# Norm statistics packed into column quarters of one PSUM bank, earlier first norm, W_proj sums in the free bank, in a gated recurrent layer with a ternary MLP

## The reference

```python
x = x + attn(layernorm(x))      # W_r, W_i: 1024 x 1024
x = x + ffn(layernorm(x))       # W_fc: 4096 x 1024, W_proj: 1024 x 4096
# attn
r = sigmoid(x @ W_r.T); i = sigmoid(x @ W_i.T)
log_a = 8 * r * log_sigmoid(lambd)
h[t] = exp(log_a) * h[t-1] + sqrt(1 - exp(2*log_a)) * (i * x)
# ffn, absmean: W / mean(|W|), rounded and clamped to -1, 0, 1
h = gelu(x @ absmean(W_fc).T)
h = layernorm(h) * ln_w + ln_b          # over 4096
y = h @ absmean(W_proj).T
```

## Time and profile before

| | us |
|---|---|
| median of three runs | 1408.09 |
| lowest run | 1407.48 |
| profiled execution | 1406.31 |
| its span (slowest core) | 1404.8 |
| spans of the eight cores | 1399.6 to 1404.8 |
| PE busy | 1260.0 |
| DVE busy | 860.9 |
| ACT busy | 746.0 |

### The profile page before, as it was taken

How to read it: one execution, slowest core, us unless ns; L and a number is a source line. 1 busy time by engine, 2 the same in 40 slices (tenths; PEclk the granted TensorE clock), 3 DMA queues, 4 the chain that set the end, 5 groups by cost and what they waited for, 6 DMA issues and landing times.

```text
span 1404.8 us, 18437 instructions; the slowest of 8 cores (1399.6 to 1404.8 us)
## 1 busy us (share of the span) xinstructions
PE 1260.0 (90%) x6180; PEld 545.5 (39%) x6180; DVE 860.9 (61%) x1554; ACT 746.0 (53%) x1155; POOL 9.1 (1%) x20
## 2 busy tenths in 40 slices
PE   2734775969999999999999999999999999999998
PEld 0211232424434444444434444444444443444443
DVE  4588676766366755677366745676457736676333
ACT  2678955861547634672647444763557354761320
POOL 2000000000000000000000000000000000000000
PEclk8866898979999999999999999999999999999999
DMA  9954763431100210002000110012000210000001
GB/s 165 312 183 112 231 196 120 151 127 46 38 1 9 58 57 1 1 24 88 10 1 8 61 53 1 1 38 83 1 0 24 61 38 1 8 24 30 1 23 38
DMA packets 32780, 85.11 MB, mean 61 GB/s; under 512 B 4016, under 2 KB 4016, under 8 KB 32688
## 3 DMA queue, kind: packets, MB, share of 16 engines
q1 hardware_dynamic: 30384, 79.74, 17.8%
q0 software_dynamic: 2304, 4.20, 2.0%
HBM read 71.34 MB, written 16.78 MB: 63 GB/s over the span
## 4 chain that ended last, share of the span: by engine, by line
PE 71%; DVE 11%; ACT 10%; issue 7%; DMA 1%; DVEq 0%; SPq 0%; ACTq 0%
PE gp L405 26%; PE yp L537 26%; PE gp L290 12%; ACT qi L607 2%; PE pS L430 1%; PE yp L225 1%; DVE acc L590 1%; PE yp L226 1%; DVE t_q L348 1%; DVE gsq_f L421 1%; PE pQ L430 1%; ACT g_f L415 1%; ACT gp L308 1%; DVE t_q L345 1%; DVE ln L274 1%
## 5 line engine op out<-in xcount | busy, mean ns | idle before, releaser
L537 PE MATMUL yp<-g_f,wp_f 128*128 128x512 bf16 x2048 | 462.7, 383 | 27.3 <-DVE cw L797 27.3
L405 PE MATMUL gp<-ln,wfc_f 128*128 128x512 bf16 x2048 | 466.4, 383 | 3.0 <-DVE wfc_f L609 3.0
L415 ACT ACTIVATE g_f<-gp 128x512 bf16<-128x512 f32 x256 | 151.9, 596 | 387.8 <-PE gp L405 385.0
L537 PEld LDWEIGHTS yp<-g_f,wp_f 128*128 128x128 fp8e4 x2048 | 201.6, 99 | 277.9 <-issue 44.1
L405 PEld LDWEIGHTS gp<-ln,wfc_f 128*128 128x128 fp8e4 x2048 | 198.5, 99 | 258.6 <-issue 31.1
L421 DVE TENSOR_TENSOR gsq_f<-g_f 128x512 bf16<-128x512 bf16 x256 | 108.6, 424 | 240.6 <-ACT g_f L415 239.9
L290 PE MATMUL gp<-ln,wr_q 128*128 128x512 bf16 x512 | 127.9, 389 | 20.9 <-DVE ln L274 12.2
L290 PE MATMUL gp<-ln,wi_q 128*128 128x512 bf16 x512 | 125.2, 389 | 1.7 <-DVE t_q L333 1.7
L302 ACT ACTIVATE gp<-gp 128x1024 f32<-128x1024 f32 x64 | 64.5, 1008 | 82.6 <-PE gp L290 82.6
L460 DVE TENSOR_SCALAR g_f<-g_f,lnw_pp 128x512 bf16<-128x512 bf16 x256 | 86.9, 347 | 24.3 <-PE pQ L430 24.3
L215 ACT ACTIVATE stx<-xb 128x512 bf16<-128x512 f32 x112 | 69.3, 619 | 34.0 <-DVE xb L356 34.0
(11 more groups left out here) (120 smaller groups left out, 1012.4 us busy)
## 6 DMA issues: line engine op xcount, KB each, us to landing
wp_f<-wp SPq DMA_DIRECT2D x41, 512.0 KB, 5.3
y<-xb SPq DMA_DIRECT2D x64, 256.0 KB, 2.2
xb<-x SPq DMA_DIRECT2D x48, 256.0 KB, 3.1
ln<-wp SPq DMA_DIRECT2D x10, 512.0 KB, 4.4
xb<-x SPq DMA_DIRECT2D x8, 512.0 KB, 6.9
wfc_f<-wfc SPq DMA_DIRECT2D x8, 512.0 KB, 18.6
g_f<-wfc SPq DMA_DIRECT2D x8, 512.0 KB, 18.4
wp_f<-wfc SPq DMA_DIRECT2D x8, 512.0 KB, 18.4
```

Of the source, the lines that this page charges most:

```text
L405: fn = lambda E, d=d: E.matmul(bank(h % 4), wfc_q[:, h * D + d * 128:h * D + (d + 1) * 128], ch(ln[k % 2], d), start=(d == 0), stop=(d == ...
L415: gelu_tok[(k, h)] = p.op("scalar", lambda E: E.activation(ch(g_sb, h), bank(h % 4), AF.Gelu))
L537: fn = lambda E, kh=kh: E.matmul(pY[b][:, :], wp_q[:, (d * NH + kh) * 128:(d * NH + kh + 1) * 128], ch(g_sb, kh), start=(kh == 0), stop=(k ...
```

## The change

- Norms 1 and 2 collect their sums as norm 3 does: `stat_pair` takes two chunks and does four matmuls with a 128 x 32 ones matrix, the two copies into rows 0 to 63 of one bank and the two squares into rows 64 to 127. Norm 3's `stat3` uses the same layout and so only `pS`.
- A new step adds the quarters: `sums_out`, one ACT copy of the bank, and `sums_mm`, two fp32 matmuls of 64 rows each, into the sum bank and the square bank. It replaces `sums3_out` and `sums3_mm`, and is new for norms 1 and 2.
- Norm 1 in the feed: the preparations run at n = 0 to 7 without pauses, the pairs at n = 2, 4, 6, 8, `sums_out` at 9, `sums_mm` at 10, `rows_var` at 11, `rows_rs` at 13, `rows_b` at 14, and the halves spread so that they end at h = 30 (from h = 15, one a group, where n is h).
- Norm 2: the pairs stand in steps e = 4 and 6, behind the last half, and behind matmul 26 of projection group 4; `sums_mm` stands behind that group.
- `cw_mm` and `cw_out` take several d at once and use `pQ`; they stand at e = 3 (d = 0), e = 5 (1 to 3) and behind the last half (4 to 7).
- The first norm of all (k = 0, norm 1) stays with `stat_mm`.

```diff
+    def stat_pair(preps, c, buf, free):
+        p.wait("tensor", *preps[c][1:], *preps[c + 1][1:], tok_ones)
+        if c == 0:
+            p.wait("tensor", *free[0])
+        for first, src in ((0, stx), (64, stq)):
+            for j in range(2):
+                sl = preps[c + j][0]
+                fn = lambda E, first=first, src=src, j=j, sl=sl: E.matmul(
+                    buf[first + 32 * j:first + 32 * j + 32, :], ones_bf[:, 0:32], ch(src, sl),
+                    start=(c == 0), stop=(c == ND - 2))
...
+        st_use[0] = st_use[1] = tk
+    def sums_out(tok_stat, buf, dst, old):
+        p.wait("scalar", tok_stat, *old)
+        return p.op("scalar", lambda E: E.activation(dst[:, :], buf[:, :], AF.Copy))
+    def sums_mm(tok, src, bS, bQ, free):
+        p.wait("tensor", tok, *free[1])
+        p.quiet("tensor", lambda E: E.matmul(bS[:, :], ones_f[0:64, :], src[0:64, :], start=True, stop=True))
+        return p.op("tensor", lambda E: E.matmul(bQ[:, :], ones_f[64:128, :], src[64:128, :], start=True, stop=True))
...  gate_step
+        if e in (4, 6):
+            stat_pair(prep2, e - 4, pS, s_free)
...
-        if e >= 3:
-            stat_mm(prep2[e - 3], e - 3, pS, pQ, s_free)
...  stat3
+        for n in (0, 2):
+            for first, src in ((0, lambda j: ch(g_sb, 4 * b + j)), (64, lambda j: ch(gsq, j))):
+                for j in (n, n + 1):
+                    at = first + 32 * (j - n)
...  feed
-                if n in PREP_AT:
-                    c = PREP_AT[n]
-                    prep1[c] = stat_prep(ln1_next, c, x_tok[(ln1_next, c)])
-                if n - 2 in PREP_AT:
-                    c = PREP_AT[n - 2]
-                    tok_st1 = stat_mm(prep1[c], c, pY[0], pY[1], y_free)
-                if n == 13:
-                    var1 = rows_var(tok_st1, pY[0], pY[1], y_free, D, rs_t, mb_t, applied)
-                if n == 15:
-                    rows1 = rows_rs(var1, rs_t)
-                if n == 16:
+                if n in (2, 4, 6, 8):
+                    tok_st1 = stat_pair(prep1, n - 2, pY[0], y_free)
+                if 0 <= n < ND:
+                    prep1[n] = stat_prep(ln1_next, n, x_tok[(ln1_next, n)])
+                if n == 9:
+                    rows1 = sums_out(tok_st1, pY[0], rs_t, applied)
+                if n == 10:
+                    rows1 = sums_mm(rows1, rs_t, pY[0], pY[1], y_free)
+                if n == 11:
+                    rows1 = rows_var(rows1, pY[0], pY[1], y_free, D, rs_t, mb_t, applied)
+                if n == 13:
+                    rows1 = rows_rs(rows1, rs_t)
+                if n == 14:
                     rows_b(rows1, rs_t, mb_t)
                     fill = apply_halves(ln1_next, 1)
-                for _ in range(-(-len(fill) // (NH - h))):
-                    fill.pop(0)()
+                if n > 14 and fill:
+                    for _ in range(-(-len(fill) // (NH - 1 - h))):
+                        fill.pop(0)()
...  k = 0
-    tail_stat(prep2, 5)
+    stat_pair(prep2, 4, pS, s_free)
     gate_tail(0, prep2, "vector")
-    tail_stat(prep2, 6)
-    st2 = tail_stat(prep2, 7)
+    st2 = sums_out(stat_pair(prep2, 6, pS, s_free), pS, rs_t, applied)
+    st2 = sums_mm(st2, rs_t, pS, pQ, s_free)
...
+    def cw_mm(*ds):
+        p.wait("tensor", *s_free[1])
+        for d in ds:
+            p.wait("tensor", *[wp_ready[i] for i in range(4 * d, 4 * d + 4)], tok_lnwb)
...  (into pQ[:, 4 * d:4 * d + 4])
+    CW_AT = {3: (0, 1), 5: (1, 4)}
...  k >= 1
-        tail_stat(prep2, 5)
+        stat_pair(prep2, 4, pS, s_free)
         gate_tail(k, prep2)
         y_part(k - 1, 4, 0, 9)
         evac(k - 1, 3)
-        tail_stat(prep2, 6)
-        y_part(k - 1, 4, 9, 20)
-        if k == 1:
-            cw_out(5, cw_mm(5))
-        st2 = tail_stat(prep2, 7)
-        y_part(k - 1, 4, 20, NH)
+        y_part(k - 1, 4, 9, 26)
+        st2 = sums_out(stat_pair(prep2, 6, pS, s_free), pS, rs_t, applied)
+        y_part(k - 1, 4, 26, NH)
+        st2 = sums_mm(st2, rs_t, pS, pQ, s_free)
         r2 = rows_a(st2, pS, pQ, s_free, D, rs_t, mb_t, applied)
```

More of the change, by code:

```diff
@@ L227, in stat_mm @@
         return st_use[sl]
+    def stat_pair(preps, c, buf, free):
[8 more added lines that the diff above has]
+                    start=(c == 0), stop=(c == ND - 2))
+                if first and j:
+                    tk = p.op("tensor", fn)
+                else:
+                    p.quiet("tensor", fn)
+        st_use[0] = st_use[1] = tk
+        return tk
+    def sums_out(tok_stat, buf, dst, old):
[5 more added lines that the diff above has]
+        return p.op("tensor", lambda E: E.matmul(bQ[:, :], ones_f[64:128, :], src[64:128, :], start=True, stop=True))
     def rows_var(tok_stat, bS, bQ, free, n, RS, MB, old):
@@ L427, in stat3 @@
             p.wait("tensor", *s_free[0], *s_free[1])
[L428 to L435, removed]
+        for n in (0, 2):
+            for first, src in ((0, lambda j: ch(g_sb, 4 * b + j)), (64, lambda j: ch(gsq, j))):
+                for j in (n, n + 1):
+                    at = first + 32 * (j - n)
+                    fn = lambda E, at=at, j=j, m=src(j): E.matmul(
+                        pS[at:at + 32, :], ones_bf[:, 0:32], m,
+                        start=(b == 0 and j < 2), stop=(b == NH // 4 - 1 and j >= 2))
+                    if first and j == 3:
+                        tk = p.op("tensor", fn)
+                    else:
+                        p.quiet("tensor", fn)
         for j in range(4):
@@ L438, in stat3 @@
             st3_tok[(k, 4 * b + j)] = tk
[L440 to L452, removed]
     def rows3(tok):
@@ L778, in wp_quant, with cw_out @@
         wp_reloads()
[L780 to L790, removed]
-                p.quiet("tensor", fn)
-        return tk
-    def cw_out(d, tk):
-        b = d % 2
+    def cw_mm(*ds):
+        p.wait("tensor", *s_free[1])
+        for d in ds:
+            p.wait("tensor", *[wp_ready[i] for i in range(4 * d, 4 * d + 4)], tok_lnwb)
+            for kh in range(NH):
+                fn = lambda E, d=d, kh=kh: E.matmul(
+                    pQ[:, 4 * d:4 * d + 4], wp_q[:, (d * NH + kh) * 128:(d * NH + kh + 1) * 128], lnwb[:, 4 * kh:4 * kh + 4],
+                    start=(kh == 0), stop=(kh == NH - 1))
+                if kh == NH - 1:
+                    tk = p.op("tensor", fn)
+                else:
+                    p.quiet("tensor", fn)
+        return tk
+    def cw_out(tk, d0, d1):
         p.wait("vector", tk)
-        tk = p.op("vector", lambda E: E.tensor_copy(cw[:, 4 * d:4 * d + 4], pY[b][:, 0:4]))
-        y_free[b] = [tk]
+        tk = p.op("vector", lambda E: E.tensor_copy(cw[:, 4 * d0:4 * d1], pQ[:, 4 * d0:4 * d1]))
+        s_free[1] = [tk]
         p.wait("vector", tk)
-        v = cw[:, 4 * d:4 * d + 4].rearrange("p (a two) -> p a two", two=2)
-        cw_tok[d] = p.op("vector", lambda E: E.tensor_tensor(cws[:, 2 * d:2 * d + 2], v[:, :, 0], v[:, :, 1], ALU.add))
+        v = cw[:, 4 * d0:4 * d1].rearrange("p (a two) -> p a two", two=2)
+        tk = p.op("vector", lambda E: E.tensor_tensor(cws[:, 2 * d0:2 * d1], v[:, :, 0], v[:, :, 1], ALU.add))
+        for d in range(d0, d1):
+            cw_tok[d] = tk
     tok_inv_p = []
@@ L826, in mid_0 @@
         def mid_0():
[L827 removed]
+            out3["toks"] = sums_out(st3_tok[(k - 1, NH - 1)], pS, rs3_t, [evac_tok[(k - 2, ND - 1)]])
         def fill_1():
[L830 removed]
+            out3["mm"] = sums_mm(out3["toks"], rs3_t, pS, pQ, s_free)
             half(k - 1, 0)
@@ L874, in fill @@
                 half(0, e - 2)
-                if e % 2 == 1:
-                    out3["cw"] = cw_mm((e - 1) // 2)
+                if e in CW_AT:
+                    out3["cw"] = cw_mm(*range(*CW_AT[e]))
             gate_step(1, e, prep2, fill, lambda: weights_step(e))
-            if e % 2 == 1:
-                cw_out((e - 1) // 2, out3["cw"])
+            if e in CW_AT:
+                cw_out(out3["cw"], *CW_AT[e])
             if e in (4, 6):
@@ L885, in gates_with_weights @@
         evac(0, 2)
-        cw_out(4, cw_mm(4))
+        cw_out(cw_mm(4, 5, 6, 7), 4, 8)
         return prep2
@@ L926, in build_nc @@
     feed_rest(k)
-    out3 = sums3_out(k, [evac_tok[(k - 1, ND - 1)]])
+    out3 = sums_out(st3_tok[(k, NH - 1)], pS, rs3_t, [evac_tok[(k - 1, ND - 1)]])
     y_part(k, 0, 16, NH)
-    rows3(sums3_mm(out3))
+    rows3(sums_mm(out3, rs3_t, pS, pQ, s_free))
     for d in range(1, ND):
```

16 lines of the change are left out of this document (3 added, 13 removed).

## The result

| | before | after |
|---|---|---|
| undisturbed executions | 1407.5 and 1408.1 us | median 1387.6 us (1386.9 to 1388.9) |
| profiled execution | 1406.3 | 1386.9 |
| its span, slowest core | 1404.8 (core 3) | 1385.3 (core 6) |
| its spans, all cores | 1399.6 to 1404.8 | 1380.5 to 1385.3 |

A forecast was written before the change was run, and what follows sets the result against it. PE, busy 90% of the span, was taken as the bound. Terms -1.6 + 3.8 - 6.4 - 2.3 - 13.7 - 1.0 = -21.2 us took the median from 1408.1 to 1387, 8-in-10 range 1376 to 1399.

The forecast's parts named there:

- the pass term: Two 64-row fp32 matmuls adding the quarters: three passes of 0.43 plus 0.1, 1.4 us a pair.
- the rival: The two 64-row fp32 matmuls run wholly side by side, 0.86 us a pair; total 1378; chance 0.12.
- A pack alone: Four 32-column statistics matmuls in different column quarters, not beside stat3's adds: 0.33 us.
- Norm 1: Feeds of k = 1 to 6: 5.77 us becomes 5.5, so -0.3 each, -1.6 for six.
- The stall's working: PE's wait for gsq in a feed moves from h = 20 to 16 and grows to 2.4 us.
- The clock: PE drops to 1.2 GHz behind 2.5 of six feed stalls, 1.5 us each: +3.8 us.
- Norm 2 and norm 3: Norm 2, k = 2 to 7: 4.1 to 3.05 us, -6.4 in all; norm 3: 1.72 to 1.4, seven times, -2.3.
- The W_proj stage: W_proj quantisation, 222 to 352 us: cw sums in free pQ end PE's copy waits; feed at 338.6, -13.7 us.
- The first failed term: W_proj quantisation: without ACT's waits of 0.76 and 1.58 for gates matmuls, all steps shift 2.3 us earlier.
- The second failed term: End of W_proj quantisation: after cw ends at 308.7, one pack and 26 matmuls finish at 314.7 us.
- The first feed: End of the k = 0 feed: 2.4 of a 3.88 us ln wait goes, next gates at full clock; -4.3 us.
- k = 0: Norm 2 while PE is idle: copy 0.6, handovers 0.2, three passes of 0.85 at 1.2 GHz; +3.3 us.

The follow-up runs named there:

- the four experiments that keep this stall: Against after: cw sums back in the projection's banks, 1398.9; full-width norm 2 at k = 0, ratio 0.9844; store behind the W_proj reload, 1383.7; wait inside fp32 pairs, 1412.9.
- the late store: Against after: store of evac(0, 1) and the x load behind it issued after the last W_proj tile's reload; 1383.7 us, ratio 0.9834 to before.
- the first two experiments: Against after: feed norm 1 as in before, 1390.1 us; only Ln and Exp (with rows_b and halves) back behind gelu(15), packs kept, 1387.2 us.

## Why the prediction was right, and where it was not

**The fp32 pair: the pass term was mis-sized.** The step said three passes of 0.43 and 0.1, since matmuls start in program order: 1.4. There are two passes side by side, 0.53 from the start of one to the start of what follows it, with 0.1 on entering: 1.16. The records at 670.68 and 670.69, then twice 671.22, show that the second pass of the first matmul does not have to run ahead of the first pass of the second. "Against: passes of one matmul must follow each other" was no argument against the rival; they do follow each other, but in step with the other's. The rival had its mechanism right and the size wrong (0.86 named, 1.16 found): its bound came from the full-row pass, and left out what entering and leaving cost. The second pass is recorded as 0.59, like a full-row one, and its 0.53 may be 0.43 and the 0.1 of leaving; the 0.1 between the first pass and the second stays unexplained. Over 19 pairs the forecast was 0.24 too dear each, 4.6 us in all. The Trainium skill ("TensorE: Matmul & The Clock Gate", Part 3) says that matmuls on different row groups run concurrently, and this trace agrees (starts 0.01 us apart); it also says that they start and end strictly in program order, and the recorded starts agree with that as well. What I had added myself, that all passes of the first come before those of the second, no page states and the trace refutes.

**A pack alone: 0.43, not 0.33.** The 0.1 of leaving the mode, seen before at `stat3`, is paid on entering too. Beside `stat3` a pack costs 0.22, as forecast. Two single packs in a feed and four in norm 2 were 0.2 and 0.4 dearer than forecast.

**Norm 1.** Terms now: packs 1.30, waits at h = 2 and 6 0.54 (0.6 forecast), the pair 1.16, the stall 2.48: 5.48, against 5.5 forecast. The stall's working (7.46 less three groups, plus 0.15) gave 2.4. The wait for the last `ln` half did go.

**The clock: right in kind.** At the lower level behind the stall were 17 of 48 feeds (eight cores, six super-tiles), each about 1.6 us longer: +0.6 per super-tile. Forecast were 2.5 of 6 at 1.5, the same. Whether a given stall of 2.48 lets the clock fall could not be told in advance, and differs from core to core in one execution. In the four experiments that keep this stall it fell in 11 to 23 of 48. Behind 1.44 (the kernel with Ln and Exp behind gelu(15)) it fell in none of the 48.

**Norm 2 and norm 3.** Norm 2 is 3.03 (four packs 1.72, 0.15 of waiting, 1.16), against 3.05 forecast: two errors of 0.4 and -0.2, and the third of the pair, cancel. Norm 3 is 1.16, -0.56 instead of -0.32. From these terms (5.77 to 5.48, 4.12 to 3.03, 1.72 to 1.16) a super-tile without a clock drop should be 1.94 shorter; 154.94 became 152.97, 1.97. The forecast was 1.67. Six times the difference is 1.8 of the 2.7 us by which the steady part beat the forecast; the clock gives 0.4, and before had one period of 155.22.

**The W_proj stage: the failed step.** Forecast -13.7, measured -10.3. The mechanism was right: the `cw` waits are gone, and undoing the bank alone costs 11.3. Two terms of the sum failed, and a third part of the miss, 0.9, is that the forecast started from core 3, whose stage took 129.3 before and not the median 128.4.

The first failed term is "steps are otherwise paced by ACT and DVE, so all shifts 2.3 earlier". ACT did shift: its waits of 0.76 and 1.58 for gates matmuls are gone. But on most cores of before these waits came to 1.5, and ACT's last read of a W_proj tile moved, in the median, by 1.3 (from 73.0 to 71.7 us behind the total of W_proj), not by 2.3. And the last tile is loaded, by SP, into a slot that ACT reads, and on SP's queue the load stands behind the store of evac(0, 1) and a load of x, which wait for DVE. On the eight cores of before the load is issued 1.7 to 3.3 us after ACT's read starts (median 2.5) and the tile is used 4.3 to 5.3 later; in after it is issued 3.3 later on every core, so 0.8 of ACT's 1.3 is spent in SP's queue, and used another 4.4 to 6.3 later; with the late store it is 1.2 and 3.7 to 4.2. On core 6 the tile was quantised at 304.76, as in before (304.83) instead of 302.5, the scan's product started at 312.24 instead of 310.0, and the next 25 projections waited 3.11 us. I had counted queues for what the change moves, and not for what it makes earlier, and I read the load on core 3, where it followed the read most closely.

The second failed term is "one pack and 26 matmuls: 314.7", which puts the 26 projections at full rate. Cores 2 and 0 of after, those projections (one record is missing on core 0):

```profile
309.75 8.68 PE L554 MATMUL yp<-g_f,wp_f 128*128 128x512 bf16 x26 [1.93 <-DVE tmp L570]
...
307.62 5.56 PE L554 MATMUL yp<-g_f,wp_f 128*128 128x512 bf16 x25 [0.72 <-DVE tmp L570]
```

On cores 0 and 3 they start 0.216 apart, and there the stage takes 115.6 and 116.0 us, where the forecast's times put it at 115.5. On the other six they start 0.26 to 0.33 apart on average, so part of them ran at the lower clock; this costs 0.9 to 2.9, the last pack stands right behind them though its square had landed 0.9 to 2.6 earlier, and the stage takes 117.3 to 118.9. In the median the clock is the larger part of the miss, some 2 us, and the late load the smaller, under 1. (Both are estimates from these rows: with the last pack right behind its square the median core would reach the feed at about 116.1.)

The late store shortened the stage by 3.8, to 14.1 less than before. That this is the size that was forecast is chance: the load goes out sooner than the forecast had it, and of the 3.8 only 1.8 are left when cores at the full clock are compared (113.7 to 114.5 us on five cores, against 115.6 and 116.0 on two). The rest is that the clock was low on three cores and not on six. It was low there without a wait of more than 0.33 just ahead, so what sets it at this place is not shown.

The Trainium skill ("DMA: Bandwidth & Descriptors", Anatomy of one DMA) says that a DMA's semaphore wait happens on the issuing sequencer, before dispatch; the section describes the GpSimd path, and this load is issued by SP. SP's rows above agree with it: the load goes out 0.92 us behind the store, at 297.62, though its slot had been read by 295.42 (294.29 + 1.13). PE's view of the end of the stage in after, core 6:

```profile
295.05 8.75 PE L554 MATMUL yp<-g_f,wp_f 128*128 128x512 bf16 x32 [3.67 <-DVE tmp L570]
303.64 3.44 PE L803 MATMUL pQ<-lnwb,wp_f 128*128 128x4 bf16 x128
...
310.73 6.70 PE L554 MATMUL yp<-g_f,wp_f 128*128 128x512 bf16 x25 [3.11 <-DVE tmp L570]
317.36 0.39 PE L237 MATMUL pS<-stx,ones_bf 128*32 128x512 bf16 x2
...
340.88 1.46 PE L431 MATMUL gp<-ln,wfc_f 128*128 128x512 bf16 x6
```

Bank 1 comes free at 295.05 (295.8 forecast), the four `cw` groups end at 307 (308.7), the feed starts at 340.88 (338.6), where it started at 352.43. What was lost lies between 307 and 317: the wait of 3.11, and 6.70 for 25 matmuls that take 5.56 at full rate. What makes the load land later when the store is ahead of it (4.4 to 6.3 us against 3.7 to 4.2) was not taken apart: two more transfers of 256 KB are under way then. The four groups of `cw` are also one stream of 3.44 here and not four of 0.8.

**The first feed: a price read from the unluckiest core.** Forecast -4.3, measured -1.3. The earlier trace rows shows the 3.88 us wait and gates at half rate behind it, on core 3, the slowest core of before. On five of the eight cores of before the stage took 98.5 to 99.5 and not 102.0. The wait was there too, but the clock did not fall. Core 1 of before, PE:

```profile
217.65 0.38 PE L290 MATMUL gp<-ln,wr_q 128*128 128x512 bf16 x1 [3.88 <-DVE ln L475]
217.87 1.89 PE L290 MATMUL gp<-ln,wi_q 128*128 128x512 bf16 x8
```

Eight matmuls in 1.89 here, where the earlier trace rows had them at half rate; so the 1.7 to 1.9 counted for the clock was nothing to gain on most cores. What the forecast said of the wait came true: it is 1.6 on three cores of after and gone on the other five. But after has something slow of its own in the same stretch, late in the first feed (core 6):

```profile
210.75 0.61 PE L458 MATMUL pS<-g_f,ones_bf 128*32 128x512 bf16 x2 [2.14 <-DVE gsq_f L447]
...
211.72 6.48 PE L431 MATMUL gp<-ln,wfc_f 128*128 128x512 bf16 x24
```

Twenty-four of these take 5.34 at full rate. In the first two experiments, where the wait is back and the clock falls behind it on all eight cores, the stage is 3.6 and 4.5 longer (medians). So the worth of the move hangs on whether the clock falls, which no row foretells, and a row of one core could not show that it varies.

**k = 0.** Forecast +3.3, measured +2.8, and the kernel with full-width statistics there confirms it: two cold passes of 1.0 stand where three of 0.85 were counted, and the copy costs 0.85 where 0.8 was.

**The sum.** Measured less forecast: -2.7 in the steady part, -0.3 in the last, -0.5 in the first stage, +3.4 in the W_proj stage, +3.0 in the first feed. The medians of the cores would make it +2.9. The rest of the agreement is which core was the slowest in each kernel.

**What could be told from no change: also a failed step.** "2% is 28 us, about what a measurement of this kernel can tell from no change" was wrong. The after runs lie within 2 us of each other and the ratio's interval is a quarter of a per cent wide on each side, so 1.4% is plainly a gain and no tie. The working had put the gain at 21.2 us, with a range whose upper end was still 9 us below before. The 0.80 for "within 2%" was given as if a time in that band could not be told from no change; the time does lie in the band, but it is a gain clear of the interval, and the working itself spoke for one.

## What to carry to other kernels

When an edit makes an engine earlier, follow each transfer that this engine releases through the queue that issues it: one store ahead of it that waits for somebody else keeps the load, and with it the gain. A stall of the bounding engine is often queue order on the engines behind it, and the same schedule need not suit the stage in which they set the pace and the one in which they don't; here writing out the order for each was worth nearly as much (18 us) as the whole change (20). Read a term of the sum from several cores: the slowest one carries its own bad luck as if it were the price. And where matmuls stand behind idle time, give them a rate from rows as well as a start.
